# Sorted experts on one core: weights as the stationary operand, fetched for each step, and the score multiplied into the rows before the scatter

## The reference, cut to what matters

```python
logits = x @ gate_w
top_val = jnp.max(logits, axis=-1, keepdims=True)
top_id = jnp.argmax(logits, axis=-1)
score = jax.nn.sigmoid(top_val)
xs = x * score
g = jnp.einsum('th,ehi->eti', xs, rt_gate)
u = jnp.einsum('th,ehi->eti', xs, rt_up)
act = jax.nn.silu(g) * u
...
```

## Time and profile before

| | |
|---|---|
| time, median of 3 runs | 590.63 us (590.25 to 591.71) |
| profiled execution: its own time | 596.14 us |
| profiled execution: span | 593.7 us |
| PE busy | 516.4 us, 87% of the span |
| DVE busy | 411.6 us, 69% |
| ACT busy | 310.4 us, 52% |
| POOL busy | 274.4 us, 46% |
| DMA | 26.24 MB, mean 44 GB/s |

### The profile page before, as it was taken

How to read it: one execution, slowest core, us unless ns; L and a number is a source line. 1 busy time by engine, 2 the same in 40 slices (tenths; PEclk the granted TensorE clock), 3 DMA queues, 4 the chain that set the end, 5 groups by cost and what they waited for, 6 DMA issues and landing times. The chain is left out here.

```text
span 593.7 us, 19118 instructions
## 1 busy us (share of the span) xinstructions
PE 516.4 (87%) x5902; PEld 365.0 (61%) x5903; DVE 411.6 (69%) x1348; ACT 310.4 (52%) x843; POOL 274.4 (46%) x693
## 2 busy tenths in 40 slices
PE   1789999999999999987927699997676789999998
PEld 0456666666666666654523355554444579999997
DVE  3888888898988888833374344542445589999974
ACT  2477777777777777652313456652333244444420
POOL 5545544465556555554320100006542588887520
PEclk9899999999999999988966899997989889999999
DMA  7900120000000000000011612221000001111000
GB/s 269 378 16 21 35 122 4 3 12 12 10 9 9 9 10 9 12 17 13 19 54 32 126 44 63 68 69 39 25 9 6 9 26 39 36 36 31 19 19 27
DMA packets 24215, 26.24 MB, mean 44 GB/s; under 512 B 4969, under 2 KB 21153, under 8 KB 23521
## 3 DMA queue, kind: packets, MB, share of 16 engines
q1 hardware_dynamic: 20688, 15.31, 8.4%
q0 software_dynamic: 3472, 10.26, 5.9%
HBM read 17.50 MB, written 7.91 MB: 43 GB/s over the span
## 5 line engine op out<-in xcount | busy, mean ns | idle before, releaser
L892 DVE TENSOR_REDUCE negm<-PS 128x4 f16<-128x512 f32 x128 | 84.7, 684 | 1.0 <-PE PS L1236 0.8
L651 ACT ACTIVATE pexp<-PS 128x512 f32<-128x512 f32 x128 | 78.3, 619 | 9.1 <-PE PS L1249 9.1
L1548 PE MATMUL PS<-w,vp 128*128 128x128 f32 x512 | 63.1, 277 | 0.0
L1548 PEld LDWEIGHTS PS<-w,vp 128*128 128x128 f32 x512 | 60.3, 193 | 0.1
L1236 PE MATMUL PS<-ktp,arena 128*64 128x128 f16 x1024 | 53.2, 227 | 4.7 <-DVE negm L892 3.5
L1263 PE MATMUL PS<-pexp,vp 128*32 128x64 f32 x2048 | 54.5, 227 | 2.1 <-ACT pexp L651 0.8
L1099 DVE SCALAR_TENSOR_TENSOR pexp<-PS,xs,oS 128x256 f32<-128x256 f32 x40 | 19.4, 484 | 50.5 <-ACT oS L752 47.5
L1449 PE MATMUL PS<-rgu,xsT 128*128 x80 | 48.4, 689 | 4.4 <-ACT xsT L757 2.6
L1236 PEld LDWEIGHTS PS<-ktp,arena 128*64 128x64 f16 x1024 | 33.0, 110 | 26.3 <-issue 15.0
L1263 PEld LDWEIGHTS PS<-pexp,vp 128*32 128x32 f32 x2048 | 34.8, 110 | 22.1 <-issue 11.7
L484 POOL TENSOR_TENSOR ve<-mv,epsc 128x1 f32<-128x1 f32 x32 | 6.1, 192 | 90.3 <-DVE mv L928 90.3
(11 more groups left out here) (225 smaller groups left out, 1317.5 us busy)
## 6 DMA issues: line engine op xcount, KB each, us to landing
xs<-sorted_x SPq DMA_DIRECT2D x40, 64.5 KB, 1.8
sorted_y<-YS SPq DMA_DIRECT2D x40, 64.0 KB, 1.6
arena<-mT SPq DMA_DIRECT2D x128, 1.0 KB
rgu<-in_rt_gate_up_dram POOLq DMA_DIRECT2D x1, 2048.0 KB, 8.0
out_dram<-X SPq DMA_DIRECT2D x32, 64.0 KB, 1.6
X<-in_x_dram SPq DMA_DIRECT2D x1, 1536.0 KB, 8.5
CK<-in_ctx_k_dram SPq DMA_DIRECT2D x1, 1536.0 KB, 11.7
CV<-in_ctx_v_swapped_dram SPq DMA_DIRECT2D x1, 1536.0 KB, 15.8
```

Of the source, the lines that this page charges most:

```text
L651: nc.scalar.activation(pexp[:, j, :], PS[:, 2 + j % 2, :], ACT.Exp).then_inc(S["exped"], 1)
L892: dve.tensor_reduce(negm[:, a.par, :, j], PS[:, j % 2, :].rearrange("p (h k) -> p h k", h=HG), AX.X, ALU.max, negate=True).then_inc(S["max ...
L1548: nc.tensor.matmul(PS[:, 6 + y.par, 0:D], z[:, y.par, e, :], w1[:, e * D:e * D + D], start=(e == 0), stop=False)
```

## The change

The gate and up weights no longer stay in SBUF. In each of the 40 steps SP reads the expert's number into a register and starts a DMA of that expert's 256 KB into one of four slots of `wst`, ahead of the load of `xs`. On PE the weights become the stationary operand: four products with 128 moving columns each give the gate and up halves already turned, so that the two transposes of the activations, their copy on ACT and one step of the pipeline go away. The score is multiplied into the rows by POOL before the scatter, once for four tiles, and the rows of `sorted_x` have 128 elements.

```diff
-        rgu = sb("rgu", [P, E * 2 * FF])
+        wst = sb("wst", [P, 4, 2 * FF])
+        expert_no = sb("expert_no", [P, NS], I32)
...
             def load_and_store(stage):
-                l, d = stage(0), stage(7)
+                l, d = stage(0), stage(6)
                 if l:
                     if not (l.turn is None and l.n < 4):
-                        sp.wait_ge(S["e_acted"], l.freed(back=4))
+                        sp.wait_ge(S["e_lifted"], l.freed(back=4))
+                    if l.turn is None and l.n == 0:
+                        sp.wait_ge(rows_known, 2)
+                    expert = sp.value_load(expert_no[0:1, ds(l.t, 1)], min_val=0, max_val=E - 1)
+                    sp.dma_start(wst[:, l.slot, :], rt_gate_up[:, ds(expert * (2 * FF), 2 * FF)]).then_inc(wst_in[l.slot], 16)
                     row = sp.value_load(rows_of[0:1, ds(l.t, 1)], min_val=0, max_val=ROWS - P)
                     sp.dma_start(xs[:, l.slot, :], sorted_x[ds(row, P)]).then_inc(xs_in[l.slot], 16)
...
-                    pool.tensor_scalar(XN2[:, 4 * k.quad:4 * k.quad + 4, D], faded[:], 0.5, 0.5, ALU.mult, ALU.add)\
+                    rows = XN2[:, 4 * k.quad:4 * k.quad + 4, :]
+                    pool.tensor_scalar(score[:], faded[:], 0.5, 0.5, ALU.mult, ALU.add).then_inc(S["k_score"], 1)
+                    pool.wait_ge(S["r_kept"], k.done())
+                    pool.wait_ge(S["k_score"], k.quad_done(2, 0))
+                    pool.tensor_tensor(rows, rows, score[:].unsqueeze(2).to_broadcast([P, TURN, D]), ALU.mult)\
                         .then_inc(S["k_score"], 1)
...
-                    nc.scalar.activation(sg[:, s.par, 0:FF], PS[:, 2 + s.par, 0:FF], ACT.Silu,
-                                         scale=xs[:, s.slot, D:DW]).then_inc(S["e_gated"], 1)
+                    nc.scalar.activation(sg[:, s.par, 0:FF], PS[:, 2 + s.par, 0:FF], ACT.Silu).then_inc(S["e_gated"], 1)
...
-                if a:
-                    act.wait_ge(S["e_down"], a.freed())
-                    act.wait_ge(S["e_act_turned"], a.done())
-                    nc.scalar.copy(act2T[:, a.par, :], PS[:, 4 + a.par, 0:FF]).then_inc(S["e_act_kept"], 1)
...
-                    dve.scalar_tensor_tensor(out=hact[:, s.par, 0, 0:FF], in0=PS[:, 2 + s.par, FF:2 * FF],
-                                             scalar=xs[:, s.slot, D:DW], in1=sg[:, s.par, 0:FF],
-                                             op0=ALU.mult, op1=ALU.mult).then_inc(S["e_acted"], 1)
+                    dve.tensor_tensor(act2T[:, s.par, :], PS[:, 2 + s.par, FF:2 * FF], sg[:, s.par, 0:FF], ALU.mult)\
+                        .then_inc(S["e_acted"], 1)
...
                 if s:
-                    e_lift = pe.snap(expert_of[s.slot], min_val=0, max_val=E - 1)
                     pe.wait_ge(S["e_acted"], s.freed())
+                    pe.wait_ge(wst_in[s.slot], 16 * (s.quad + 1))
                     pe.wait_ge(S["e_turned_kept"], s.done())
-                    nc.tensor.matmul(PS[:, 2 + s.par, :], xsT[:, s.par, :], rgu[:, ds(e_lift * (2 * FF), 2 * FF)],
-                                     start=True, stop=True).then_inc(S["e_lifted"], 1)
+                    for i in range(4):
+                        last = nc.tensor.matmul(PS[:, 2 + s.par, i * P:i * P + P], wst[:, s.slot, i * P:i * P + P],
+                                                xsT[:, s.par, :], start=True, stop=True)
+                    last.then_inc(S["e_lifted"], 1)
...
-                if a:
-                    pe.wait_ge(S["e_act_kept"], a.freed())
-                    pe.wait_ge(S["e_acted"], a.done())
-                    for i in range(2):
-                        last = nc.tensor.transpose(PS[:, 4 + a.par, i * P:i * P + P],
-                                                   hact[:, a.par, 0, i * P:i * P + P], identf)
-                    last.then_inc(S["e_act_turned"], 1)
```

More of the change, by code:

```diff
@@ L133, in flamingo_gated_two_layers @@
         CV = sb("CV", [P, NT * D])
-        VALL = sb("VALL", [P, NT * DW])
+        VALL = sb("VALL", [P, NT * D])
         CW = [P, P, P, P, E, E, NS, 1, SEQ, TURN * E, HG]
@@ L176, in twin @@
             return spare[:, k * 2 * D:(k + 1) * 2 * D].rearrange("p (s d) -> p s d", s=2)
-        XN2 = VALL.rearrange("p (t d) -> p t d", d=DW)
+        XN2 = VALL.rearrange("p (t d) -> p t d", d=D)
+        score = sb("score", [P, TURN])
         XNT = sb("XNT", [P, NT * P])
@@ L213, in flamingo_gated_two_layers @@
         squares = pexp
-        hact = pexp.rearrange("p (c i) t -> p c i t", c=2)
-        zeros = sb("zeros", [P, SPARE * DW])
-        xs = sb("xs", [P, 4, DW])
+        zeros = sb("zeros", [P, SPARE * D])
+        xs = sb("xs", [P, 4, D])
         xsT = sb("xsT", [P, 2, P])
@@ L353, in flamingo_gated_two_layers @@
         xs_in = [sem(f"xs_in{c}") for c in range(4)]
-        for n in "turned turned_kept lifted gated acted act_turned act_kept down kept".split():
+        wst_in = [sem(f"wst_in{c}") for c in range(4)]
+        for n in "turned turned_kept lifted gated acted down kept".split():
             S["e_" + n] = sem("e_" + n)
@@ L425, in _ @@
                 tail = sp.value_load(cnti[0:1, 0, e:e + 1], min_val=0, max_val=ROWS - P)
-                sp.dma_start(sorted_x[ds(tail, P)], zeros[:, 0:DW]).then_inc(tails_zero, 16)
+                sp.dma_start(sorted_x[ds(tail, P)], zeros[:, 0:D]).then_inc(tails_zero, 16)
             sp.wait_ge(rows_known, 1)
@@ L477, in _ @@
                           *((ginit4[:, q * D:q * D + D], g_init) for q in range(CT)),
-                          *((binB4[:, q * D:q * D + D], b_in) for q in range(CT)), (rgu, rt_gate_up))
+                          *((binB4[:, q * D:q * D + D], b_in) for q in range(CT)))
             def step(stage):
@@ L540, in step @@
                     pool.wait_ge(S["k_placed"], o.quad_done(2, 1))
-                    pool.wait_ge(S["k_score"], o.quad_done())
-                    pool.wait_ge(S["r_kept"], o.done())
+                    pool.wait_ge(S["k_score"], o.quad_done(2, 1))
                     pool.indirect_dma_start(out=sorted_x,
@@ L729, in gates_in_drain @@
                     shared_gate(1, 1)
-                    act.wait_ge(late_in, 16 * 17)
+                    act.wait_ge(late_in, 16 * 16)
                     scaled_by_gate(rdn[:, 0:512], 2)
@@ L747, in sorted_step @@
             def sorted_step(stage):
-                l, f, s, a = stage(0), stage(2), stage(3), stage(4)
+                l, f, s = stage(0), stage(2), stage(3)
                 if s:
@@ L1032, in _ @@
             then(dve.tensor_reduce(texpf[:], tcmp[:, :, 0:E - 1], AX.X, ALU.add))
+            dve.tensor_copy(expert_no[:], texpf[:]).then_inc(rows_known, 1)
+            dve.wait_ge(rows_known, 2)
             digits = texpf[:].rearrange("p (s k) -> p s k", k=4)
@@ L1089, in sorted_step @@
             def sorted_step(stage):
-                l, s, d = stage(0), stage(3), stage(6)
+                l, s, d = stage(0), stage(3), stage(5)
                 if d:
@@ L1107, in sorted_step @@
                         .then_inc(sq_summed, 1)
-            walk(dve, NS, 7, sorted_step, early=plugs_early)
+            walk(dve, NS, 6, sorted_step, early=plugs_early)
             def pick_plugs(c):
@@ L1129, in depooled @@
                     dve.wait_ge(late_ready, 6)
-                    dve.wait_ge(S["e_act_turned"], Tile(NS - 1).done())
                 dve.wait_ge(S["c_placed"], f.freed())
@@ L1220, in _ @@
             quad_credit(pe, ("k_ranked", 1))
-            credit(pe, *((n, 1) for n in ("h_down e_turned e_act_turned e_lifted e_down c_depooled c_placed l_hnT_done "
+            credit(pe, *((n, 1) for n in ("h_down e_turned e_lifted e_down c_depooled c_placed l_hnT_done "
                                           "l_mixed l_xnT_done l_routed l_spread l_mask_turned l_summed").split()),
@@ L1443, in sorted_step @@
             def sorted_step(stage):
-                f, s, a, b = (stage(i) for i in range(2, 6))
+                f, s, b = (stage(i) for i in range(2, 5))
                 if s:
-                    e_lift = pe.snap(expert_of[s.slot], min_val=0, max_val=E - 1)
                     pe.wait_ge(S["e_acted"], s.freed())
+                    pe.wait_ge(wst_in[s.slot], 16 * (s.quad + 1))
                     pe.wait_ge(S["e_turned_kept"], s.done())
-                    nc.tensor.matmul(PS[:, 2 + s.par, :], xsT[:, s.par, :], rgu[:, ds(e_lift * (2 * FF), 2 * FF)],
-                                     start=True, stop=True).then_inc(S["e_lifted"], 1)
+                    for i in range(4):
+                        last = nc.tensor.matmul(PS[:, 2 + s.par, i * P:i * P + P], wst[:, s.slot, i * P:i * P + P],
+                                                xsT[:, s.par, :], start=True, stop=True)
+                    last.then_inc(S["e_lifted"], 1)
                 if f:
@@ L1457, in sorted_step @@
                     pe.wait_ge(S["e_kept"], b.freed())
-                    pe.wait_ge(S["e_act_kept"], b.done())
```

(1 more changed line is left out.)

19 lines of the change are left out of this document (9 added, 10 removed).

## The result

| | before | after |
|---|---|---|
| median of 4 runs | 591.17 us (590.25 to 596.27) | 625.32 us (622.88 to 627.62) |
| ratio, 95% interval | | 1.054 (1.0472 to 1.0607) |
| profiled execution: its own time, span | 596.14, 593.7 us | 627.6, 625.8 us |

The changed kernel is slower by about 34 us. The forecast was 614.5 us with a range of 603 to 628: the side is as forecast and the time lies in the range, but the likeliest number is 11 us too low.

What follows compares the result with a forecast made beforehand. The prediction saw a PE-ACT round with SP 97% full, and SP bounding after the change. A loop end 23.2 us later plus 1 us of register work made 24 us, so 614.5 us from the median, range 603 to 628.

Steps and rivals of the forecast that it cites:

- SP as the bound: Sorted loop: SP's issue list, already 97% full, would set the pace at 3.05 us a step against some 2.0.
- The price of 1.11 us: SP's added read, register work and DMA per step, priced from eight tail DMAs ahead of the loop; bounds 0.61 and 1.49.
- 1 us for the register instruction: One extra REGISTER_ALU in each SP step, taken at 0.03 us a step, 1 us in all.
- The start: Ahead of the loop: SP's first load at 311.36 is now weights, so `xs` and PE are 1.11 us late.
- The 4.87 us should not appear in the sum: Stall at 340.25 for a late `xs`: SP runs ahead and PE catches up; if not absorbed, 4.87 us come on top.
- (c): Rival: the 4.87 us stall is not absorbed, or transfers grow each other's landing by as much: 619.5 us, chance 0.08.
- (a): The forecast itself: SP bounds the loop at about 3.05 us a step, giving 614.5 us, chance 0.68.
- The load of tile 39 lands at 427.9 (1.8): Loop's end: the last `xs` load, leaving SP at 426.1, would take 1.8 us to land.
- The tail from that landing to the last `YS`: Loop's end: transpose, copy, lift, silu, product, down and last copy would run from 427.9 to 431.9.
- (b): Rival: PE falls to the lower clock in the loop and becomes the bound, up to 624 us, chance 0.12.
- (d): Rival: SP's new group is cheap, so PE and ACT's round decides; faster at 586.5 us, chance 0.07.
- PE's side, hidden: Loop: lift 1.01 us against 1.12, PE and ACT's round 1.87 us, all hidden behind SP's 3.05 a step.

Runs made afterwards that it cites:

- e1: The kernel before, plus one read of the expert's number and an unused 8 KB DMA in each SP step: 630.64 us, ratio 1.0585.
- e3: The changed kernel with the weights' reads and DMAs issued by POOL instead of SP: 596.63 us, ratio 1.0026.
- e5: The changed kernel with the stores of `YS` issued by ACT instead of SP: 615.16 us, ratio 1.0271.
- e9: The changed kernel with a fixed expert, so the 256 KB DMA stays and the read with its register work goes: 605.47 us, ratio 1.014.
- e8: The changed kernel with POOL's broadcast of the table for layer two cut to 4 of its 32 parts: 624.33 us, ratio 1.0425.
- e10: The changed kernel with 12 unused half-precision 128x128 products in each PE step, to hold the clock up: 624.25 us, ratio 1.0436.
- e4: The changed kernel with all weights resident in SBUF and POOL copying the expert's columns to `wst`, no weight DMA: 584.64 us, ratio 0.984.
- e2: The kernel before, plus one read of the expert's number and an unused 256 KB DMA in each SP step: 631.17 us, ratio 1.0567.

## Why the prediction was right, and where its size was off

**SP as the bound** was right, and e1, e3 and e5 show it from three sides: the group alone costs the loss, the group elsewhere costs nothing, and 0.62 us less on SP are 0.62 us less in a step. The trace has the steps that were forecast: 3.02 us against 2.95, a turn of 12.26 against 12.18, PE's idle time at the transpose of `xs`, no shift before 300 us. The price of 1.11 us from the earlier trace rows holds; e9 gives 1.13. The TENSOR_LOAD stayed at 0.27 us, so the sum by the Trainium skill's floor of about 600 ns for a `tensor_load` ("DMA: Bandwidth & Descriptors", latency and other measured facts), below 609, would have been further off. That floor is not seen here, but a read with its register work, 0.68, is close to it.

**Where 8 us were missed.** The last `YS` came at 440.85. The forecast says 431.9, with its 1 us for the register instruction 432.9. The difference of 8 us, in terms of its own sum:

- The start is 0.6 later (311.97 against 311.36). The turns are as forecast: with its register instruction a turn was put at 12.18 + 4 x 0.03 = 12.30 us, and 12.26 were measured, 0.3 less over seven turns.
- "The 4.87 us should not appear in the sum": this step failed. SP runs ahead of PE by at most four tiles, that is about 12 us, and the stall grew to 8.54 us. SP was stopped for 3.2 us, and a loop in which SP has nothing to spare can't make them up. That is the condition that the forecast itself named, and the first half of (c), on top of (a). e8, without the stall, has a wait of 0.3 us. The other half of (c), that the transfers of weights grow the landing, is not needed for it: e1, with 8 KB a step, has a stall of 7.25 us and a wait of 3.1.
- "The load of tile 39 lands at 427.9 (1.8)": it took 4.0 us from issue to use, 2.2 more. The 1.8 was a median from a quieter loop; the median now is 2.2. Why this last load took more is open: in e8 and e10 it was used after 2.35 and 1.97 us.
- The tail from that landing to the last `YS` was put at 4.0 us and took 6.0, with products at the lower clock (the lift 1.92 us, down 1.22): 2.0. In e8 and e10, at the full clock, it took 4.3 and 4.9.

These come to 0.6 - 0.3 + 3.2 + 2.2 + 2.0 = 7.7 us, about what was missed. That the time still lay inside the range owes something to luck: its upper end was put there for (b) and (c), which together had a chance of 0.20, and it was half of (c) that came. The remaining 2 us between the 34 us of the medians and the 32.1 of the traces is the spread of the runs: the profiled execution of before lay 5 us over its median, that of after 2.3.

**The rivals.** (b), the lower clock as the bound, was wrong for the pace (e10: 12.25 us a turn with the clock held up) and right that the clock falls. It cost only where SP's time does not cover it. In the changed kernel the clock stayed at 1.00 from 375 to 390 us, with waits of 0.40 to 1.63 us for `xs` in its steps, and was 0.89 in the next two windows. (c) was true in kind, as said. (d), the faster side, needed a group of at most a fifth of 1.11 us. It fell; but e3 and e4 show what it described, the kernel with that group out of SP's list.

**PE's side, hidden.** The lift was put at 1.01 us and takes 1.13 to 1.16, no less than the old one of 1.12. It made no difference, since SP covered it. The forecast's round of 1.87 us is 1.79 around 329 us and 1.91 in e4.

## What to carry to other kernels

Add up the issuing engine's list for one step, reads into registers and waits included, before moving a load into a loop: it has no busy row, and the engines that starve by it show their idle time at a DMA that looks slow. If the list is as long as the step, put the group on an engine that is idle there, or keep the data resident and let that engine copy. And count a stall as absorbed only if the issuing engine never has to wait for it: an engine that is full, as SP here, can't make up what it waits.

## What the runs showed of the hardware

- A DMA on SP whose address comes from a number in SBUF costs 1.11 to 1.13 us of SP: 0.27 for the read, some 0.4 of register work, and the issue, 0.34 as a row and 0.46 as a difference between kernels.
- The size of the transfer did not matter to the issuer: 8 KB and 256 KB both gave a loop of 129 to 130 us (e2, e1).
- PE at the lower clock changed nothing in the pace of a loop that waits for SP (12.26 and 12.25 us a turn), and cost 1 to 2 us at the tail, where PE is alone on the path (e10, e8).
- With the same 256 KB a step the core moved 131 GB/s when SP issued the loads and 201 GB/s when POOL did (e3), so the 131 were no limit of the DMA engines.
- Two such groups on POOL started 1.78 us apart at the closest (e3, from 350 to 395 us), against 1.11 us on SP.
